# A state-space layer whose step sizes are spread over the array three steps ahead of the scan in place of two

## The reference

```
xz = x @ W_in.T; u, z = split(xz)                  # 512 channels each
u_c = silu(conv4(u) + conv_b)
dt_r, Bm, Cm = split(u_c @ W_x.T, [16, 32])
dt = softplus(dt_r @ W_dt.T + b_dt)                # a step size for each channel and token
A = -exp(A_log)                                    # 512 x 16
h = exp(dt_t * A) * h + (dt_t * u_t) * B_t         # over the 128 tokens, each channel and state
y = h . C_t + u_c * D
out = (y * silu(z)) @ W_out.T
x = layernorm(x + out)
```

## Time and profile before

| | before |
|---|---|
| median of three runs | 3147.79 us |
| lowest and highest | 3145.26, 3156.16 us |
| the profiled execution: time, span | 3160.88, 3159.1 us |
| TensorE, VectorE, ScalarE, GpSimd busy over the span | 2758.4, 1647.7, 1440.2, 1390.0 us |
| TensorE's granted clock over the span | 0.932 of full |

### The profile page before, as it was taken

One profiled execution on the slowest core, in us unless ns is written; L12 is line 12 of the kernel. 1 busy time (PEld: TensorE's weight loads), 2 busy tenths in 40 slices (PEclk: granted clock), 3 DMA queues, 4 the chain that ended last, 5 costly groups with the idle time before them and its releaser, 6 DMA issues.

```text
span 3159.1 us, 71137 instructions
## 1 busy us (share of the span) xinstructions
PE 2758.4 (87%) x25057; PEld 2151.1 (68%) x25057; DVE 1647.7 (52%) x3584; ACT 1440.2 (46%) x4586; POOL 1390.0 (44%) x1628
## 2 busy tenths in 40 slices
PE   5888888558989997987995988999996996999999
PEld 5777777445666665664664776787785664777888
DVE  2888889774436664553113773333333223555643
ACT  3555656353446665663334882323222233773310
POOL 1666666561346665553334562332332222663321
PEclk9998999688999998997997998999996998999999
DMA  2000000110000000033112020000006111010100
GB/s 80 2 3 2 2 2 2 30 40 29 1 26 15 17 29 2 0 109 103 46 47 84 1 84 15 8 10 10 10 18 235 38 34 54 1 47 25 55 9 19
DMA packets 75145, 106.16 MB, mean 34 GB/s; under 512 B 11024, under 2 KB 54672, under 8 KB 74656
## 3 DMA queue, kind: packets, MB, share of 16 engines
q1 hardware_dynamic: 68960, 86.68, 8.3%
q0 software_dynamic: 5952, 16.26, 1.6%
HBM read 88.50 MB, written 14.42 MB: 33 GB/s over the span
## 4 chain that ended last, share of the span: by engine, by line
PE 53%; POOL 5%; DVE 4%; issue 3%; ACT 3%; DMA 1%; SPq 1%; DVEq 0%; ACTq 0%; POOLq 0%
PE up_ps L2423 5%; PE e_out_ps L2441 5%; PE t_ps L618 3%; PE s_ps L604 3%; PE bank_a L1492 3%; PE bank_b L1492 3%; POOL probs L523 2%; PE up_ps L2417 2%; ACT probs L742 2%; PE bank_a L566 2%; PE bank_d L655 2%; PE frame_ps L1571 2%; PE bank_b L1508 2%; PE bank_d L574 2%; PE bank_a L1508 2%
## 5 line engine op out<-in xcount | busy, mean ns | idle before, releaser
L523 POOL TENSOR_TENSOR probs<-probs,inv 128x512 f32<-128x512 f32 x320 | 328.1, 1040 | 280.1 <-DVE inv L847 279.7
L3335 POOL TENSOR_TENSOR hc<-h,bc 128x1024 f32<-128x1024 f32 x128 | 301.7, 2358 | 191.1 <-DVE h L3599 174.4
L742 ACT ACTIVATE probs<-s_ps,negmax 128x128 f32<-128x128 f32 (+1 forms) x768 | 297.7, 415 | 7.8 <-DVE negmax L807 6.3
L3599 DVE TENSOR_TENSOR_SCAN h<-da,dbu_ps 128x1024 f32<-128x1024 f32 x128 | 292.4, 2284 | 10.3 <-DVE dbu_ps L3611 4.8
L618 PE MATMUL t_ps<-ident,probs 128*128 128x128 f32 x1280 | 208.7, 286 | 59.3 <-POOL probs L523 50.9
L618 PEld LDWEIGHTS t_ps<-ident,probs 128*128 128x128 f32 x1280 | 139.6, 142 | 126.5 <-POOL probs L523 60.8
L3419 PE MATMUL dta_ps<-dt,a_spread 32*128 32x128 f32 x2048 | 165.0, 304 | 46.7 <-ACT da L3546 25.6
L3611 DVE TENSOR_TENSOR dbu_ps<-dbu_ps,bc 128x1024 f32<-128x1024 f32 x128 | 155.7, 1217 | 78.5 <-PE dbu_ps L3424 78.2
L3546 ACT ACTIVATE da<-dta_ps 128x1016 f32<-128x1016 f32 x128 | 130.3, 1018 | 145.2 <-PE dta_ps L3419 144.8
L3419 PEld LDWEIGHTS dta_ps<-dt,a_spread 32*128 32x128 f32 x2048 | 138.9, 205 | 70.3 <-ACT da L3546 30.9
L807 DVE TENSOR_REDUCE negmax<-s_ps 128x4 f32<-128x1024 f32 (+1 forms) x128 | 156.6, 1223 | 44.9 <-PE s_ps L604 43.0
(11 more groups left out here) (504 smaller groups left out, 6825.1 us busy)
## 6 DMA issues: line engine op xcount, KB each, us to landing
cT<-in_ctx_turned SPq DMA_DIRECT2D x32, 256.0 KB, 2.6
w_down<-in_L_ffn_w SPq DMA_DIRECT2D x8, 1024.0 KB, 12.1
w_up<-in_L_ffn_w SPq DMA_DIRECT2D x8, 1024.0 KB, 13.4
c_in<-in_ctx SPq DMA_DIRECT2D x16, 256.0 KB, 2.8
w_gate<-in_L_ffn_w SPq DMA_DIRECT2D x8, 512.0 KB, 6.4
w_up<-in_L_ffn_w SPq DMA_DIRECT2D x8, 512.0 KB, 9.2
w_down<-in_L_ffn_w SPq DMA_DIRECT2D x8, 512.0 KB, 9.1
w_gate<-expert_rows_out SPq DMA_DIRECT2D x8, 512.0 KB, 7.1
```

Source lines behind the costliest of these rows:

```text
L523: pool.tensor_tensor(probs[:, u % 2, i], probs[:, u % 2, i], inv[:, u % 2, HB * i:HB * (i + 1)].unsqueeze(2).broadcast_to([P, HB, W]), ALU ...
L742: last = act.activation(probs[:, u % 2, i, k, :], src, ACT.Exp, bias=negmax[:, u % 2, at], accum_out=sums[:, u % 2, at])
L3335: pool.tensor_tensor(hc[:, s % 4], h[:, s % 2], bc[:, j, 1, :].unsqueeze(1).broadcast_to([P, 2 * G, P]), ALU.mult).then_inc(hc_ready.sem, 1)
L3599: dve.tensor_tensor_scan(flat(h[:, s % 2]), flat(da[:, s % 4]), dbu_ps[s % 2][:, :, :, :].rearrange("p i g t -> p (i g t)"), 0.0, ALU.mult ...
```

## The change

TensorE's burst at step s now spreads the step sizes of step s + 3, with the inputs of step s + 1 as before. ScalarE's decay at step s is that of step s + 3. Ahead of the first sequence both make step 2 as well. Nothing else is changed; the buffers stay as many as they were.

```diff
             def unit(b, j, first, left):
                 for s in range(H):
-                    spread_out(half_at(b, j, s + 2, left), half_at(b, j, s + 1, left))
+                    spread_out(half_at(b, j, s + 3, left), half_at(b, j, s + 1, left))
...
             spread_out((0, 0, 1), (0, 0, 0))
+            spread_out((0, 0, 2), None)
             pe.wait_ge(rest_in.sem, rest_in.base + 32)
...
             def unit(b, j, first, left):
                 for s in range(H):
-                    ahead = half_at(b, j, s + 2, left)
+                    ahead = half_at(b, j, s + 3, left)
...
             decay((0, 0, 1))
+            decay((0, 0, 2))
             every_sequence(act, unit)
```

## The result

The changed kernel takes 3315.4 us, the median of four runs (3310.2 to 3326.2), against 3146.5 us before, over four runs (3137.4 to 3156.2). The ratio is 1.0541, with a 95% interval of 1.0498 to 1.0583: 170 us slower. I had forecast 3228 us, between 3200 and 3258. The side was right; the 80 us that I forecast are half of what came.

The account below looks back on a forecast made before the run. TensorE with its round trips was taken to bound the layer at full clock. Longer bursts 99.7, hidden -16, sequence 14 +4, sequence 15 +1, preparation +2, clock -11 made 80 us on 3147.8: 3228 us, between 3200 and 3258.

Parts of the forecast that it names:

- What bounds the layer: In the layer at full clock, TensorE with its round trips sets the pace; no scan waits for a decay, saving 0.
- The shared rows: Both kinds in a TensorE burst share 64 rows: about 2.05 us in place of 1.17, 99.7 us over 14 sequences.
- What is hidden of it: Longer bursts fill TensorE's waits for the scan and `uc`: 16 us off, at most 23; sequence 14 adds 4 us.
- The clock: TensorE idles less between bursts, so its clock falls less often: 11 us off, between 0 and 22.
- The last sequence and the preparation: Sequence 15 has five longer bursts with more room: 1 us; preparation gains a spread and a decay: 2 us, once.
- Rows that don't matter: First rival: the array's rows don't matter and bursts stay at 1.17 us; 3150 us, no change; chance 0.05.
- loads that are no longer hidden: Third rival: matmuls on a busy row group wait for weight loads, bursts 5.0 us; some 3570 us; chance 0.02.
- the faster one: Second rival: bursts stay short, earlier decays close TensorE's gaps and its clock no longer falls; 3126 us; chance 0.02.
- The fourth: Fourth rival: VectorE hides the longer burst, leaving 3.5 us a sequence; 3178 us with the clock's full return; chance 0.06.
- if the clock stayed low and the sequences came to 40 us: One of the listed signs, in the layer's sequences, that would prove the prediction wrong; no chance given.
- What the profile was to show: Bursts 2.05 us, full-clock sequence 38 us, layer +80 us, VectorE's input wait some 150 us, clock above 0.91.

Follow-up runs that it names:

- the moved sum: Kernel before (lead of two), with the second chunk's sum over the states issued at step 4, ahead of `project_u`, in place of step 5: 3133.9 us, ratio 0.9947.
- the rows apart: The change (lead of three), with the two steps swapping rows in every second chunk of 128 channels, so a burst's parts use different halves: 3149.2 us, ratio 1.0000.
- the run with 64-row matmuls: Kernel before (lead of two), each spread matmul contracting over all 64 rows of its step in place of 32, using the whole array: 3244.3 us, ratio 1.0299.

## Why the prediction was half right

**What bounds the layer: right.** By the estimate above the full-clock sequence grew by 5.9 of the 7.1 us, so TensorE sets the pace once its bursts are longer. How narrowly it did before I hadn't seen: the moved sum shows VectorE nearly level with it at 31.5 us. The scan waited for no decay before, and with the rows apart the longer lead was worth 0 (ratio 1.0000).

**The shared rows: right.** 2.05 us forecast, 2.05 us measured.

**What is hidden of it: the right size, in part by luck.** Fifteen sequences at 5.9 us more are 88 us, and my terms for them (99.7 - 16 + 4) made 88. But the waits that I had named gave little of the 16. In the first 14 sequences, which the term counts, TensorE's wait for the scan was 8.2 us and is 5.2, and its matmuls' wait for `uc` was 2.1 us and is gone (the 5.0 us that I read were the wait of the weight loads). Other parts came from places that I had put at nothing or left out: the wait for the decay behind the first burst fell from 1.18 to 0.97 us, and the `step_sizes` matmuls run inside a burst, from 512.00 us on, where before they stood behind it.

**The clock: the step that failed.** I wrote that TensorE has less idle time between bursts, "so it should fall to the lower level less often", and took 11 us off. I had read the falls of before as following idle time alone, and had not asked what else the trace showed of them. The 15 sequences lie 652.8 - 15 x 37.6 = 89 us over a full-clock pace; with 10 for the loop's turns as before, the clock costs 79 us in place of 22. The term is +57, not -11. The split between this term and the one before it is an estimate: with the 38.67 us of the run with 64-row matmuls, whose bursts are 0.1 us longer than the change's, it would be 104 and +41. Either way the sign of the clock's term was wrong, and it is the larger part of the miss. Had the whole array worked, most of the return would have come: in that run the 15 sequences lie 591.2 - 580.1 = 11 us over its full-clock pace, 10 of them for the loop.

**The last sequence and the preparation.** 39.18 against 30.27 us is 9 us where I had 1; its clock was 0.63, which I had left out. The preparation I had at +2; the first scan starts 2.5 us earlier than before, because the burst ahead of it did (59.25 against 61.70 us). What moved that burst is not shown. The added spread comes behind it and is counted in the first sequence.

Together: 88 + 57 + 9 - 2.5 = 151 us, against 88 - 11 + 1 + 2 = 80.

**The rivals.** Rows that don't matter, and loads that are no longer hidden, are both refuted by the burst of 2.05 us, and so is the faster one, which needed short bursts. The fourth, in which VectorE hides the longer burst and 3.5 us a sequence are left, is refuted by the 5.9. My list of what would prove me wrong had "if the clock stayed low and the sequences came to 40 us"; the clock fell further and they came to 43.5, but I had not given that case a price.

**What the profile was to show.** The length of the bursts, the scan's idle time, the stages behind and the full-clock sequence (37.6 us, an estimate, against 38) came as written. The waits for the scan were halved and didn't go. VectorE's wait for its inputs is 233 us, not 150, the layer's stretch grew by 151 us, not 80, and its clock fell where I had it rise.

## What to carry to other kernels

In this kernel small matmuls that contract over 32 rows ran beside one another only where they stood on different rows of the array (a burst of 1.18 us against 2.05). A change of software pipelining by one step can turn that around without touching a matmul, since the parity that keeps two streams apart goes with the distance between them. Check which rows meet in the new order before asking what the new lead hides. And where a longer lead is wanted, first look for who waits for it; here nobody did, and the half per cent came from filling a wait of TensorE.

## What the runs showed of the hardware that I had not expected

TensorE's clock fell from 2.4 to 1.2 GHz behind 8.00 us in which the engine was never idle, where the bursts used half of its rows. The mean granted clock was 0.80 with 95% busy where they stood on 64 rows, 0.98 with 94% busy on 128 rows, for as many instructions in the same order at the same pitch. The Trainium skill, TensorE: Matmul & The Clock Gate, "Part 1: The HAM clock gate (the "warmup" mystery)", has the clock follow how busy the engine has been. By busy time these two runs should not have differed; they lie 187 us apart.

Matmuls on one group of rows kept a pitch of 0.11 us with new weights for each, in bursts of 2.05 us. The same page, "The mechanism", lists that weight loads overlap running matmuls only where the row groups differ, while its text ahead of the list also lets them go ahead into the background weight buffer; these bursts agree with the second and not with the first.
